# Attention walks: VectorE runs the links of each step of the maxima's chain in one row, the four additions behind them

## What is computed

```python
e = leaky_relu(a_src[src] + a_dst[dst], 0.2)              # 8 heads
e_max = segment_max(e, dst, num_segments=N)
e_exp = exp(e - e_max[dst])
denom = segment_sum(e_exp, dst, num_segments=N)
msg = h[src] * (e_exp / (denom[dst] + 1e-16))[:, :, None]
out = segment_sum(msg, dst, num_segments=N)
```

## Time and profile before

| | us |
|---|---|
| median of 3 runs | 6938.87 |
| lowest and highest | 6933.76, 6942.06 |
| the profiled execution | 7003.0, its span 7001.2 |
| first walk, chunks with gathers (from its second weighing group on) | 181 to 831 |
| second walk, the same | 1531 to 2173 |
| third walk, the same | 2587 to 3229 |
| fourth walk, the same | 3399 to 4049 |

### The profile page before, as it was taken

How to read it: one execution, slowest core, us unless ns; L and a number is a source line. 1 busy time by engine, 2 the same in 40 slices (tenths; PEclk the granted TensorE clock), 3 DMA queues, 4 the chain that set the end, 5 groups by cost and what they waited for, 6 DMA issues and landing times. The chain is left out here.

```text
span 7001.2 us, 80027 instructions
## 1 busy us (share of the span) xinstructions
PE 4860.9 (69%) x19231; PEld 3375.8 (48%) x19232; DVE 3942.7 (56%) x8585; ACT 2369.7 (34%) x5719; POOL 2991.1 (43%) x2932
## 2 busy tenths in 40 slices
PE   2677749637775947775577756888799555467999
PEld 2444526425444734443344433444587433356777
DVE  3555643446667246666366665666424788787333
ACT  1333412123333223433344324555321122265333
POOL 2555432445552045553555526666100577643000
PEclk8777859868887968887788868899899766687999
DMA  4454414234442024443444422121001799954000
GB/s 117 139 159 155 118 42 137 89 96 142 138 147 66 14 91 141 137 146 92 126 145 137 144 50 35 30 31 30 18 13 42 270 376 369 324 189 142 10 14 23
DMA packets 543459, 819.11 MB, mean 117 GB/s; under 512 B 87966, under 2 KB 421967, under 8 KB 542839
## 3 DMA queue, kind: packets, MB, share of 16 engines
q0 software_dynamic: 140832, 376.78, 19.2%
q1 hardware_dynamic: 396388, 432.93, 19.1%
q10 hardware_dynamic: 5907, 5.92, 0.3%
HBM read 658.06 MB, written 157.71 MB: 117 GB/s over the span
## 5 line engine op out<-in xcount | busy, mean ns | idle before, releaser
L783 POOL DMA_INDIRECT l_edges_stage<-l_h_rows,src_t x832 | 802.7, 965 | 687.0 <-issue 223.7
L1096 PE MATMUL l_edges_ps_sum<-l_edges_msg,l_edges_hot 128*128 128x264 f32 x1664 | 602.7, 505 | 262.3 <-DVE l_attn_acc L925 182.3
L2510 POOL DMA_INDIRECT l_edge_kv<-l_kv_rows,src_t x416 | 479.1, 1152 | 668.3 <-POOLq L2417 517.7
L2938 POOL DMA_INDIRECT l_gate_edges_srow<-l_gate_src_rows,l_gate_edges_idx x512 | 487.1, 951 | 330.9 <-issue 141.7
L3074 PE MATMUL l_gate_edges_ps<-l_gate_edges_wide,l_gate_edges_hot_lo 128*128 128x500 f32 x1024 | 507.9, 639 | 103.8 <-issue 77.0
L1096 PEld LDWEIGHTS l_edges_ps_sum<-l_edges_msg,l_edges_hot 128*128 128x128 f32 x1664 | 360.0, 241 | 423.4 <-DVE l_attn_acc L925 258.8
L2563 PE MATMUL l_edge_ps_q<-l_q_q,l_edge_hot 128*128 x832 | 338.0, 577 | 324.9 <-issue 193.5
L783 POOL DMA_INDIRECT l2a_edges_stage<-l2a_h_rows,src_t x416 | 401.9, 966 | 338.4 <-issue 114.4
L783 POOL DMA_INDIRECT l2b_edges_stage<-l2b_h_rows,src_t x416 | 401.7, 966 | 331.7 <-issue 115.5
L2563 PEld LDWEIGHTS l_edge_ps_q<-l_q_q,l_edge_hot 128*128 128x128 f32 x832 | 230.1, 289 | 432.7 <-issue 387.2
L1096 PE MATMUL l2a_edges_ps_sum<-l2a_edges_msg,l2a_edges_hot 128*128 128x272 f32 x832 | 304.5, 510 | 159.3 <-DVE l2a_sums_acc L925 101.1
(11 more groups left out here) (784 smaller groups left out, 10845.6 us busy)
## 6 DMA issues: line engine op xcount, KB each, us to landing
l_edge_e<-e_rows SPq DMA_DIRECT2D x416, 128.0 KB
l_val_rows<-l_edge_vj SPq DMA_DIRECT2D x104, 512.0 KB
l_agg_stage<-l_val_rows SPq DMA_DIRECT2D x52, 1024.0 KB, 5.5
l_edges_rel_b<-rel_rows SPq DMA_DIRECT2D x52, 512.0 KB
l_edges_ea<-in_edge_attr SPq DMA_DIRECT2D x48, 512.0 KB
e_rows<-l_edges_e_s SPq DMA_DIRECT2D x48, 512.0 KB
l_experts_w<-in_L_ffn_w SPq DMA_DIRECT2D x32, 512.0 KB, 5.1
l_gate_edges_lo_b<-l_gate_edges_lo_rows SPq DMA_DIRECT2D x64, 256.0 KB
```

Source lines behind the costliest of these rows:

```text
L783: nc.gpsimd.indirect_dma_start(out=stage[:, c % SL, u, :], out_offset=None, in_=h_rows, in_offset=bass.IndirectOffsetOnAxis(ap=K.src_t[:, ...
L1096: nc.tensor.matmul(ps_sum[u][:], hot[:, g, u, :], msg[:, g % 2, u, :], start=True, stop=True).then_inc(summed, 1)
L2510: nc.gpsimd.indirect_dma_start(out=kv[:, m, u, :], out_offset=None, in_=kv_rows, in_offset=bass.IndirectOffsetOnAxis(ap=K.src_t[:, n * EB ...
L2938: nc.gpsimd.indirect_dma_start(out=srow[:, n % 4, u, :], out_offset=None, in_=src_rows, in_offset=bass.IndirectOffsetOnAxis(ap=idx[:, n * ...
```

## The change

Only the places of the calls `add(u)` in the three steps change. Before, they stood between the links; now the links of a step come first, and the four additions of the group behind them. The waits of the links on each other stay where they were.

```diff
                     nc.vector.tensor_tensor_scan(local[:, 1, :], cut_f, lgT, NEG, ALU.add, ALU.max).then_inc(dv, 1)
-                    add(0)
                     nc.vector.tensor_tensor_scan(local[:, 0, :][:, ::-1], cut_r, lgT[:, ::-1], NEG, ALU.add, ALU.max).then_inc(dv, 1)
-                    add(1)
                     dve.wait_ge(dv, c * STEP + SEG2 + 2)
...
                     nc.vector.tensor_tensor(placed[:], cols.unsqueeze(1).to_broadcast([P, CK, 2]), bcast(K.of_tile[:], 2), ALU.mult).then_inc(ends_made, 1)
-                    add(2)
-                    add(3)
+                    for u in range(GR):
+                        add(u)
...
                     nc.vector.tensor_tensor_scan(top[:, m, :][:, ::-1], link_r, run[:][:, ::-1], NEG, ALU.add, ALU.max).then_inc(dv, 1)
-                    add(0)
                     dve.wait_ge(dv, c * STEP + SEG2 + 4)
...
-                    for u in range(1, GR):
+                    for u in range(GR):
                         add(u)
...
                     nc.vector.tensor_copy(init[:], ps_init).then_inc(dv, 1)
-                    add(0)
                     dve.wait_ge(dv, c * STEP + SEG2 + 5)
                     nc.vector.tensor_tensor_scan(fwd[:], cut_f, lgT, init[:, 0:1], ALU.add, ALU.max).then_inc(dv, 1)
-                    add(1)
                     dve.wait_ge(f_made, c + 1)
...
                     nc.vector.tensor_tensor_scan(seg_max[:][:, ::-1], cut_r, fwd[:][:, ::-1], init[:, 1:2], ALU.add, ALU.max).then_inc(maxed, 1)
-                    add(2)
-                    add(3)
+                    for u in range(GR):
+                        add(u)
```

## The result

The changed kernel takes 7036.43 us, median of 4 runs (7035.59 to 7045.25), against 6939.9 us for the kernel before beside it (4 runs, 6933.76 to 6942.06): a ratio of 1.0143, interval [1.0131, 1.0155], so 97 us more. The forecast was 7064 us, +125. A few executions further down took 2 to 23% longer than the others of the same kernel, at a lower granted clock (6305 and 7603 us of 29, 7181 of 17, 7487 of 5); no ratio uses them, and the one profile that fell on such an execution, of the changed kernel without most gathers, is not read.

What follows compares the result with a forecast made beforehand. No one engine is full; VectorE bounds chunks without gathers, and with them TensorE's results, held until gather runs drain, make it wait. Terms 14 + 0 + 21 + 90 = 125 us gave 7064 us, range 6990 to 7150.

Steps and rivals of the forecast that it cites:

- the waits before L866: Tops step's first link: 292.5 us idle in four walks, TensorE's results being announced only when the gather run has drained.
- 53 chunks with this wait and 39 with another: Of 92 gathering chunks, 53 have their long wait before L866, at 5.5 us each; the others before L882 or earlier.
- Price (1): VectorE's own time per chunk from additions waiting for each other: ends +0.82, tops +0.33, maxima +0.64 us.
- Price (2): TensorE's start waits for the first addition, which comes later: +0.50 us in tops, +0.98 in maxima.
- Ends, 0 in gathering chunks: Ends step: its 0.82 us goes into 5.5 us of waiting before L866, cost 0; 32 us if cover missing in 39 chunks.
- Tops, 21 us: Tops step: 0.40 us in each of 53 chunks where L866 starts free of gathers, 21 us; 0 in the other 39.
- Maxima, 90 us: Maxima step: TensorE starts 0.98 us later and everything behind it too, in 92 gathering chunks, 90 us.
- rival B: Maxima step: the delay pushes L1082 into a gather-run stall, 2.1 us more in half of 92 chunks; 7161 us, chance 0.12.
- my lower bound: Maxima step: at least the 0.64 us of VectorE's time per gathering chunk, if TensorE catches up, 59 us.
- Eight chunks without gathers, 14 us: Last two chunks of each walk: nothing covers VectorE's longer steps, 1.8 us each, 14 us.
- A: The gathers pace everything, so delays vanish except in the 8 chunks without gathers: +14 us, 6953 us, chance 0.10.
- C: TensorE's small matmuls wait for the links, not the scatter, so the change helps: 57 us, 6882 us, chance 0.04.

Runs made afterwards that it cites:

- without most gathers: Gathers of all but each walk's first three chunks left out: kernel before 6308.92 us (0.9083), changed kernel 6382.91 us (0.9186), both against 6946.24 us.
- held condition: Visits to a chip in which the unedited kernel before took about 6945 us; TensorE's results came late during gather runs.
- free condition: Visits to a chip in which the same unedited kernel before took about 6172 us (6173.1 in its rerun).
- the maxima step alone: Kernel before with only the maxima step's additions moved behind its links: 7003.36 us, 1.0081 in the held condition; 1.0001 in the free condition.
- the answers ahead of the scatter: Changed kernel with TensorE's small matmuls answering the next step put before their group's scatter: 7110.43 us, 1.0245 against the kernel before, held condition.

## Why the prediction was right, and where its sizes were off

**What bounds it.** The reading of the waits before L866 stands: in the held condition they end with the gather run, and with the gathers the waits go. What I did not see is that this holds in one of two conditions only. And my split into 53 chunks with this wait and 39 with another does not stand: in the held trace of before 78 of 88 gathering chunks wait over 1 us before L866, 79 before L882 and 69 before both. The zero of the ends step is thus better covered than I argued, and the 21 us of tops rest on a count that is wrong.

**Price (1), VectorE's length.** Predicted +0.82, +0.33, +0.64; measured +0.54, +0.17 and 2.84 - 2.42 = +0.42. The three terms took 0.12 us between dependent instructions and 0.60 between additions. The additions stand 0.58 apart. The product L855 starts 3269.73 - 3269.30 = 0.43 behind the second scan, which is busy 0.39: 0.04, not 0.12. The 0.12 came from L866 to L868, and it is 0.39 for 0.27 there still; for the wide scans it is not so. By the rule of the Trainium skill as I read it (VectorE: DVE Perf Modes, The DRAIN you can't avoid) the steps would have kept their length. They grow by 1.1 us, so it does not carry over from the copies on which that section measured it to additions behind each other, 0.58 against 0.35 where nothing is waited for, though the gap is less than I had taken. The same section adds that a next instruction that is not held starts earlier, and the 0.35 agrees with that.

**Price (2), TensorE's start.** Predicted +0.50 in tops and +0.98 in maxima. In the chunk without gathers the first addition of tops stands 3274.27 - 3273.16 = 1.11 behind its first link, after 0.69: +0.42. In maxima it moved by 0.85 in the median chunk with gathers. The error is the 0.12 us between dependent links again and, in maxima, the 0.28 that I took from the copy to the scan, which is 0.20.

**Ends, 0 in gathering chunks.** Right in the held condition: +9 us in all, of which 0.9 in each of the 8 chunks without gathers makes 7. In the free condition that cover is gone, and it costs 20 us; I had priced a missing cover (32 us), but not for this reason.

**Tops, 21 us.** Only a subtraction speaks to it: 97 - 58 - 9 = 30, with its share of the eight chunks without gathers and whatever the parts do together. It agrees with a term whose count of chunks was wrong, which is luck in part.

**Maxima, 90 us.** This is the mis-sized term. With the step alone 58 were measured, some 50 of them in the 92 gathering chunks: 0.54 a chunk and not 0.98. The usual chunk does nearly what the term says (+0.94 to the next step). Not in the term were the long stretches that before already had here, 6 of 88 chunks; in the trace of the maxima step alone they are nearly gone, which gives 0.2 a chunk back: rival B with the other sign. The changed kernel's two traces, though, keep 6 and 4 somewhat shorter ones, and give back 0.1 to 0.2. Another 0.1 or so may be taken in by the next long wait. These would account for some 0.3 of the 0.4 us; the traces are of single executions, before's is 63 us off its median, and so the cause of the shortfall is argued and not shown. In the same chunks my lower bound for this step was 59, so the 50 lie below it.

**Eight chunks without gathers, 14 us.** Measured +19, seen as two distances between last scans (`seg_max`) a walk, 148.1 us before and 167.3 now over the four (from weighing to weighing, 142.4 and 164.0, it is 22). The sum is near, its working is not: VectorE's own 1.1 us each explain 9. Measured from a chunk's first weighing to the next one's, the first such chunk of a walk grows by 1.4 us on average at full clock before and after, and the second by 4.0 (69.9 to 85.7 us over the four walks). In the second TensorE ran at full clock before and does not now (0.76, 0.77, 0.84 and 0.73 in the four walks), and in walk 3 VectorE waits for it twice:

```profile
3246.83:3264.41 17.58, 11.45 (x57) 6.44 (x53) 15.76 (x40) 11.17 (x33) 0.00 (x0) 1.00 0.09 30
```

```profile
3284.73:3305.87 21.14, 13.71 (x46) 8.37 (x43) 16.36 (x39) 10.90 (x33) 0.00 (x0) 0.84 0.07 25
```

```profile
3298.91 0.16 DVE L879 COPY l2a_edges_init<-l2a_edges_ps_w 128x2 f32<-128x2 f32 x1 [1.14 <-PE l2a_edges_ps_w L1072]
...
3303.18 0.29 DVE L894 TENSOR_TENSOR l2a_edges_last_max<-l2a_edges_ps_w,last_t 128x128 f32<-128x128 f32 x1 [0.80 <-PE l2a_edges_ps_w L1077]
```

The first window is of the kernel before (0.09 and 30 behind the clock are DMA), the other rows are of the changed one. There was no cover for TensorE's late start either, and I had priced only VectorE there.

**The sum.** The maxima term is 40 too high (90 against 50 in the gathering chunks). The others are too low: ends by 2, the chunks without gathers by 5, and tops, by what is left over, by 5. That makes 28, 125 against 97. So the total is nearer than its largest term, because errors of both signs met.

**The rivals.** A is false in the held condition (+97) and true for the maxima step in the free one. B is false for the change: L894 waits 1.57 us in the chunk shown, not 3, and its wait is over 3 us in 3 of 88 chunks of one trace and in none of the other. What B describes, a result held until the run has ended, did happen with the answers ahead of the scatter. C is false: L1077 stands 3039.16 - 3034.95 = 4.21 behind the copy, later than before (3.40), with its link 0.8 earlier.

**The signs named.** Additions in fours at 0.6: yes, 0.58. The last scan 0.87 behind the copy: 0.71. L879 to L894 4.9: 4.84. Two chunks after the gathers +3 to 4 us: 5.9 in walk 3, 4.8 on average. Walk 3's gathering chunks +25 to 35: the traces show 12, in a pair that understates; from the timed runs some (97 - 19) / 4 = 20 a walk are left, still under the range.

## What to carry to other kernels

When work is moved behind a chain to let the chain run free, look at who waits for the moved work. Here each addition frees the PSUM tile of a matmul, and the chain's answer stands behind two such matmuls in TensorE's order: the last link started 0.8 us earlier and the answer came 0.7 to 0.9 us later. Which of several releases counts depends on how fast the waiting engine is at that moment, so read the clock of the stretch before choosing the one to protect; and a delay seen in the usual chunk is a price only after the rare long ones and the next long wait have been looked at.

## What the runs showed that I had not expected

The same program takes about 6940 or about 6172 us, 12% apart, and keeps to one of them for a whole visit; one chip showed both in different visits. Of the 837 us between the two traces of the kernel before, 636 lie in the four walks (from the first L890 of each to its last) and some 200 outside them, 140 of these behind the fourth. Without most gathers the walks take 2048 us, as little as in the free condition with them (2109), but the rest of the kernel keeps its held length, 4244 us against 4256 with the gathers and 4055 in the free condition. So held results during runs of gathers are not all that differs. Edge-walk chunks with gathers take 26.7 or 20.3 us, while gathers have the same pace (1.26 us); in the held condition a result of TensorE that falls into a run of gathers reaches VectorE up to 5.9 us after the start of its matmul, when the run has ended, and in the free one after 0.4 us. What sets the condition stays open: nothing in the two programs differs, and no run here changed it but by leaving the gathers out. The granted clock differs with it, 0.81 to 0.82 over the held executions of the kernel before and 0.86 to 0.87 over the free ones, and no run tells whether as a cause or as a consequence.

With a change on VectorE alone TensorE's granted clock moved: from 0.82 to 0.76 over the gathering chunks of walk 3, and from 1.00 to between 0.73 and 0.84 in the second chunk without gathers of each walk. It is no rule for the whole kernel. In the gathering chunks of walks 1 and 2 the two traces show the same 0.78 and 0.82, and in the free condition the maxima step alone has a higher clock in the walks than before (0.91, 0.95, 0.98 and 0.98 against 0.90, 0.93, 0.93 and 0.94). What part of the price is paid through the clock was not separated.
